# Second aggregation of a graph network kernel: edge tiles 1925 to 2050 counted on TensorE, 1075 tiles gathered in place of 1200

## What is computed

```
# L0: two SAGE convolutions with mean aggregation
deg_inv = 1 / max(deg, 1)                       # 0 where deg is 0
h = relu(x @ Ws1 + (segment_sum(x[src], dst) * deg_inv) @ Wn1 + b1)
h = h @ Ws2 + (segment_sum(h[src], dst) * deg_inv) @ Wn2 + b2
x = layernorm(x + h)
# L1: messages over the edges
ef  = (relu(edge_attr @ We1 + be1) @ We2 + be2) * sigmoid(edge_weight @ Wt + bt)
msg = relu(concat([x[src], ef]) @ Wm1 + bm1) @ Wm2 + bm2
out = layernorm(x + segment_sum(msg, dst) + x)
```

## Time and profile before

| what | us |
|---|---|
| median of 3 runs | 8275.95 |
| lowest and highest | 8274.34 and 8285.98 |
| profiled execution, its own time | 8290.47 |
| its span in the trace | 8288.8 |
| second stage in it, first gather to last window sum | about 2497 to 4070 |

### The profile page before, as it was taken

The page is one execution under the profiler, slowest core; times in us unless marked ns, Lnnn a source line. Parts: engine busy times, 40 slices in busy tenths (PEclk is TensorE's granted clock), DMA queues, the critical chain, the costliest instruction groups (busy, mean ns, idle before and its releaser), DMA issues.

```text
span 8288.8 us, 106834 instructions
## 1 busy us (share of the span) xinstructions
PE 6509.1 (79%) x34084; PEld 4100.4 (49%) x34084; DVE 4750.7 (57%) x8573; ACT 2462.6 (30%) x2998; POOL 5925.0 (71%) x5857
## 2 busy tenths in 40 slices
PE   5778777777776788887678888878888888888887
PEld 4555555444444555555444444444444444444444
DVE  8988877676755555555354444444444444444454
ACT  2111111111111000000134444444444444444444
POOL 7777665555547777777577777777777777777776
PEclk8889888888888999898799999999999999999998
DMA  4466666676758889898644444444444444444443
GB/s 122 154 201 223 228 231 227 232 240 219 249 190 285 290 298 309 303 318 305 216 124 125 130 127 127 129 123 128 126 128 126 129 127 130 125 128 129 128 129 98
DMA packets 598838, 1523.91 MB, mean 184 GB/s; under 512 B 157137, under 2 KB 290917, under 8 KB 587014
## 3 DMA queue, kind: packets, MB, share of 16 engines
q1 hardware_dynamic: 411075, 1133.17, 40.2%
q0 software_dynamic: 187200, 383.76, 16.7%
HBM read 1374.92 MB, written 141.47 MB: 183 GB/s over the span
## 4 chain that ended last, share of the span: by engine, by line
POOL 37%; issue 11%; PE 1%; DMA 1%; DVE 0%; POOLq 0%; ACT 0%; SPq 0%; DVEq 0%; ACTq 0%
POOL messages_rows L1704 37%; DMA messages_rows<-y_d,src_idx 1%; PE messages_p_msg L1785 1%; PE messages_p_msg L1788 0%; POOLq L1701 0%; DMA messages_sums<-in_message_base 0%; PE messages_win L1743 0%; PE messages_win L1761 0%; PE messages_win L1544 0%; DVE messages_below L1905 0%; DVE messages_parts L1895 0%; PE messages_p_edge L1800 0%; DVE messages_piece_stats L1559 0%; ACT messages_product L1833 0%; ACT L1536 0%
## 5 line engine op out<-in xcount | busy, mean ns | idle before, releaser
L1704 POOL DMA_INDIRECT messages_rows<-y_d,src_idx x3125 | 3190.2, 1021 | 1001.1 <-issue 944.5
L1110 POOL DMA_INDIRECT sum_x_rows<-in_x,sum_x_edges x1525 | 1568.5, 1029 | 855.8 <-PE sum_x_win L1200 428.3
L1900 DVE SCALAR_TENSOR_TENSOR messages_gated<-messages_p_edge,be,messages_gate 128x1024 f32<-128x1024 f32 x391 | 502.0, 1284 | 2138.8 <-PE messages_p_edge L1800 1039.3
L1110 POOL DMA_INDIRECT sum_z_rows<-z_d,sum_z_edges x1200 | 1165.0, 971 | 473.5 <-issue 419.2
L1785 PE MATMUL messages_p_msg<-messages_rows,identity 128*128 128x512 f32 x1564 | 963.2, 702 | 630.1 <-DMA messages_rows<-y_d,src_idx 611.5
L1788 PEld LDWEIGHTS messages_p_msg<-Wm_e,messages_gated 128*128 128x128 f32 x6250 | 937.6, 215 | 454.5 <-issue 454.5
L1212 PE MATMUL sum_x_build<-sum_x_key_hot,sum_x_low_hot 128*128 128x490 bf16 (+2 forms) x2900 | 837.0, 375 | 228.6 <-DVE sum_x_counts L1408 223.9
L1788 PE MATMUL messages_p_msg<-Wm_e,messages_gated 128*128 128x128 f32 x6250 | 929.2, 298 | 0.0
L1232 PE MATMUL sum_z_p_loaded<-sum_z_split,sum_z_counts 128*128 128x384 bf16 x2744 | 790.9, 346 | 155.1 <-DMA sum_z_split<-z_parts_d 149.9
L1820 ACT ACTIVATE messages_parts<-messages_p_msg 128x1024 bf16<-128x1024 f32 x391 | 399.7, 1022 | 1572.1 <-PE messages_p_msg L1788 1572.1
L1408 DVE SCALAR_TENSOR_TENSOR sum_x_counts<-sum_x_counts,sum_x_build 128x980 f32 (+3 forms) x635 | 647.8, 1020 | 360.6 <-PE sum_x_build L1212 348.5
(11 more groups left out here) (274 smaller groups left out, 9360.5 us busy)
## 6 DMA issues: line engine op xcount, KB each, us to landing
sum_x_split<-x_parts_d SPq DMA_DIRECT2D x392, 675.5 KB
sum_z_split<-z_parts_d SPq DMA_DIRECT2D x392, 675.5 KB
messages_when<-in_edge_weight SPq DMA_DIRECT2D x391, 512.0 KB
messages_attr<-in_span_attr SPq DMA_DIRECT2D x391, 256.0 KB, 3.1
counts_d<-sum_x_counts SPq DMA_DIRECT2D x28, 3136.0 KB
sum_z_counts<-counts_d SPq DMA_DIRECT2D x56, 1568.0 KB, 7.7
messages_rows<-y_d,src_idx POOLq DMA_INDIRECT x3125
sum_x_rows<-in_x,sum_x_edges POOLq DMA_INDIRECT x1525
```

Source lines behind the costliest of these rows:

```text
L1110: nc.gpsimd.indirect_dma_start(out=rows[:, s % depth, j, :], out_offset=None, in_=table, in_offset=bass.IndirectOffsetOnAxis(ap=edges[:, b ...
L1704: nc.gpsimd.indirect_dma_start(out=rows[:, g % SPAN_DEPTH, j, :], out_offset=None, in_=d["y"], in_offset=bass.IndirectOffsetOnAxis(ap=src_ ...
L1900: nc.vector.scalar_tensor_tensor(gated[:, g % SPAN_GATEDS, :], p_edge[:], t.be2[:, 0:1], gate[:, g % SPAN_GATES], ALU.add, ALU.mult).then_ ...
```

## The change

Tiles 1925 to 2050 are taken from the gathered to the counted ones. Their keys cover ten nodes, so a key table has 980 columns for 784 and the two build matmuls have 490 for 392. `sum_z_` builds 19 blocks for 13 and gathers 215 groups for 240. The tiles are to be built within 188 slots for 212, and 22 pieces for 20 are in the flat part.

```diff
-RUNS = (..., (1600, 1, 6), (1925, 1, 8))
+RUNS = (..., (1600, 1, 6), (1925, 1, 8), (2050, 1, 10))
...
     first = make_plan(m, 0, 1600, 28, 14, 290, SPACING)
-    second = make_plan(m, 1600, 1925, 13, 20, 212, SPACING_SECOND, first)
+    second = make_plan(m, 1600, 2050, 19, 22, 188, SPACING_SECOND, first)
```

More of the change, by code:

```diff
@@ L29 @@
 BANK_NODES = 5
-RUNS = ((300, 5, 5), (600, 3, 6), (750, 3, 8), (1050, 3, 10), (1200, 2, 8), (1500, 2, 10), (1600, 1, 6), (1925, 1, 8))
+RUNS = ((300, 5, 5), (600, 3, 6), (750, 3, 8), (1050, 3, 10), (1200, 2, 8), (1500, 2, 10), (1600, 1, 6), (1925, 1, 8), (2050, 1, 10))
 LONGEST = max(run for _, run, _ in RUNS)
```

## The result

| | before | after |
|---|---|---|
| median us, lowest to highest, 4 runs each | 8279.48 (8274.34 to 8285.98) | 8490.48 (8481.37 to 8494.56) |
| profiled execution, its own time | 8290.47 | 8494.56 |

The ratio of the times is 1.0253 with a 95% interval of 1.0235 to 1.0271. The change costs 211 us: slower, as forecast, inside the range, but 84 us above the forecast of 8406. Between the two profiled executions the spans differ by 203.9 us (8492.7 for the earlier trace rows).

What follows compares the result with a forecast made beforehand. Second-stage slots were bound closely together by gathers (6.37 us), TensorE's program order (6.78) and the chunk stream; 27 + 753 + 805 + 118 = 1703 us for 1573, so 130 us more: 8406 us, 8 in 10 range 8265 to 8500.

Steps and rivals of the forecast that it cites:

- start: Second stage from the first gather to the first pass: 26 us as now plus 1 us for the larger tables.
- first 16 passes: Slots 4 to 82 of the second stage: nine one-block passes at 44 us and seven two-block at 51, 753 us.
- slots 82 to 189: Late second stage with more builds per slot: 50 slots of 7.2 us and 57 of 7.8, 805 us.
- end: After slot 189: POOL's last 90 gathers, 114 us, and 4 us for the last window, 118 us.
- the gap: Between two passes, from last to next first product matmul: 9.2 or 10.7 us, holding half the counts and the first chunk.
- The lengths: Early passes without their gaps: 33.8 us with one block, plus 1 for piece traffic in the distance; 40 us with two.
- The marks of the second count halves: Sign that the forecast is right: these marks stand 43 to 53 us apart for the first 16 passes.
- the 0.95 or more: Sign that the forecast is right: DMA engines busy at least 0.95 in the first 16 passes, at about 350 GB/s.
- ten-node slots: Last 57 slots of slots 82 to 189, 2.2 tiles each: 7.8 us a slot; above 9 would show the forecast wrong.
- Ten-node part as slow as the first stage: Rival: ten-node slots take 9.7 us as TensorE and VectorE wait in turn, 108 us more, 8514 us; chance 0.14.
- Added work fits idle time: Rival: passes at the transfers' 41 us, late slots at the gathers' 6.37, 90 us less, 8186 us; chance 0.17.
- The stream is faster when asked: Rival: chunks move at 407 GB/s, early passes take 35.7 us, 571 for all sixteen, 8224 us; chance 0.06.

Runs made afterwards that it cites:

- run 3: Changed kernel with second-stage chunk loads, after the first three, cut to one slice of seven: 8375.29 us, 115 less than the changed kernel.
- run 8: Kernel before the change with chunk loads after the first three cut to one slice of seven: 8263.66 us against 8290.96 beside it.
- run 4: Changed kernel with VectorE's second-stage addition of counts cut to 14 of 98 slices: 8376.92 us, 114 less than the changed kernel.
- run 6: Changed kernel with the products of its last six blocks cut from 98 matmuls to 2 each, builds and chunk loads kept: 8472.39 us, 18 less.

## Why the prediction was right and where it was off

**Direction and place.** Right. Moving 125 tiles takes away 25 slots and lengthens the others. The stage took 208 us more (1781 for 1573), all else 4 us less (203.9 - 208).

**The terms**, from the cuts in the windows above:

| term | forecast | measured |
|---|---|---|
| start | 27 | 44 |
| first 16 passes | 753 | 825 |
| slots 82 to 189 | 805 | 787 |
| end | 118 | 125 |
| sum | 1703 | 1781 |

By the starts of the 17th and the 28th pass, which is what the forecast's terms meant, the last three are 815, 792 and 130: the sixteen passes missed by 62, and 10 us of the 72 in the table come from where I cut.

**Start: missed by 17.** I took it as 26 us and 1 us for the larger tables. In slot 2 VectorE runs a chain of short instructions for the places of the blocks (L280 to L312), 10.5 us here (2528.16 to 2538.62) and 9.9 in the kernel before (2521.29 to 2531.20). Everything that TensorE needs of VectorE stands behind it. Before, five builds stood ahead of the first product matmul at 2522.85, and TensorE met the chain behind it, in the first pass; now eight do, and it meets the chain ahead of the pass. TensorE's two waits, before and after, and part of the chain after:

```profile
2532.76 0.66 PE L1196 MATMUL sum_z_win<-sum_z_hot,sum_z_rows 128*128 128x64 f32 x2 [8.42 <-DVE sum_z_hot L976]
...
2541.90 0.81 PE L1212 MATMUL sum_z_build<-sum_z_key_hot,sum_z_low_hot 128*128 128x392 bf16 x2 [11.99 <-DVE sum_z_counts L1408]
...
2528.80 2.67 DVE L286 MEMSET sum_z_counts<- 1x44 f32 x20
```

So 12 of the 17 us are a wait that the kernel before has too, in its first pass (44.0 us long, for 37.0 now). The forecast left it out: its start is that of before, and its passes are copies of later ones.

**First 16 passes: the step that failed is the gap.** The lengths hold: 35.3 us for a forecast of 33.8 + 1, and 39.3 for 40. The gap was taken as 9.2 and 10.7 us, read at two passes at the start of the stage, with the reason that "half of the counts and the first chunk have to land in it". It was 13.9 behind both kinds, so the gaps cost 9 x 4.7 + 7 x 3.2 = 65 us, and the lengths came 2 or 3 us under: together the 62. Two things were wrong with it. The two rows were not typical: they hold no step of a piece, and over its first 16 passes the kernel before had 11.6 and 11.8, which alone makes 9 x 2.4 + 7 x 1.1 = 29 us. And the reason was wrong, so I let it stay where it grows. With the chunks cut to a seventh the gap did not move, in the changed kernel (run 3) or in the one before (run 8); with short additions it fell by 2 us (run 4). The other 36 us, 2.2 in each gap, come with the slots' other work: a gap now holds five builds where it held three. By the table of gaps TensorE's idle time in them is the same 5.3 us, of which more now ends with an addition (4.6 for 2.2) and next to none with a chunk (0.04 for 1.7), and its busy time grew by 2.3 us. Part of that is the clock and not the work. At the higher level the busy times would be some 6.3 x 0.84 = 5.3 and 8.6 x 0.73 = 6.3 us, an estimate from the table's rows, so about 1 us more work and about 1.3 us at the lower clock. No run separates the two. Of the length of a pass with two blocks I had the number and not the reason either: I set it by the transfers, and it is TensorE's own work. The marks of the second count halves came 46 to 55 us apart, for 43 to 53. The DMA engines stood at 0.86 over the stretch, not at the 0.95 or more that I had named as the sign: by run 3 transfers set only the passes with one block, 9 x 35.3 = 318 of the 815 us.

**Slots 82 to 189: right in sum, in part by luck.** 787 us for 805, 7.3 us a slot; VectorE was busy 558.58 of 787 us, 71% (forecast 60 to 70). TensorE's waits moved from chunks to additions as said. But ten-node slots were not the longer ones: timed by window sums they took 7.2 us from slot 131 on, where I had 7.8, and the eight-node slots before them 7.6, where I had 7.2. The two errors have opposite signs, some 19 us too little and 32 too much. The run with eight-node keys does not settle why, since it also moved tiles.

**End: 125 for 118.** A small miss.

**The rivals.** *Ten-node part as slow as the first stage* (9.7 us a slot): its time, 8514, is nearer to the result than the forecast, but its mechanism is excluded, these slots took 7.3. *Added work fits idle time:* excluded, late slots are 7.3 and not 6.37; run 6 shows the little that is true of it, TensorE's own matmuls for the six blocks are worth 18 us because VectorE's turn comes out under them. *The stream is faster when asked:* passes stood 49.2 and 53.2 us apart, not 35.7, and with six sevenths of every chunk load left out (run 3) the kernel still takes 96 us more than before (8375.29 for 8279.48), so a faster stream of chunks could not have made the change a gain. The Trainium skill, DMA: Bandwidth & Descriptors, section Bandwidth, has 425 GB/s for 16 MB at once and 341 for 1 MB; the first 16 passes moved 294 GB/s and 395 in 6 us of a gap, so no run tests the higher figure over a pass.

**Where the 211 us come from.** Not from one thing. The parts that runs measured, each alone:

- Waits for chunks that gathers covered before: cutting chunks gives 27 us in the kernel before and 115 in the changed one, nearly all of it in the nine early passes with one block. The difference is 88 us. Run 8 shows why: before, waits for gathered rows took the place of the waits for chunks.
- The builds of the 125 new tiles (key table, build columns, addition): 68 us by the time, of which 16 lie in the first sixteen passes, where the edit changes nothing; some 50 us.
- The products of the six new blocks: 18 us.

These are some 156 us, of single runs, and need not add. Some 55 us stay open. Three candidates are argued only: the 325 old tiles are built in fewer slots, the granted clock in the first part is 0.87 for 0.90 and in the early gaps 0.73 for 0.84, and at the start the wait described above is 3.6 us longer (12.0 for 8.4).

Single runs can be compared more closely by the stage alone, from the first gather to the last window sum in each trace, 1780.6 us in the changed kernel and 1571.7 in the one before. By it the cuts in the changed kernel took 128 us (chunks), 112 (additions), 266 (both), 20 (products) and 66 (builds), and the cut of the chunks in the kernel before took 41; the two orders turned round cost 47 and 65 us, and the second of them 21 in the kernel before. The difference that rests on two runs, 128 for 41, is 87 us and so the same as above.

## What to carry to other kernels

When one engine's pace (here POOL's gathers) covers the waits of the others, taking work from that engine removes the cover too: price every wait it hid, not just the work added. The same cut of the transfers was worth 27 us with the cover and 115 without it, because under the cover 103 us of waits for gathered rows came up in place of 141 us of waits for chunks. A term used sixteen times should be read as a mean over the stage and not at its first two places, and it is explained only when one knows all the work that stands in it: a wait for a transfer ended my gap, but it hid under the other work as soon as that grew. Where two engines take turns on one buffer, taking work from one of them gives back only part of it: 53 us of TensorE's matmuls gave 20, and some 360 us of VectorE's additions (489 to 127) gave 114. A stall that both kernels have can move from one term of the sum to another, as the chain of short instructions did here.

## What the runs showed that was not expected

Turning two orders round that looked wrong in the trace made the kernel slower each time: additions before key tables, 49 us; chunk loads ahead, 69 us, and 26 us in the kernel before. The granted clock fell to its lower level inside the gap shown above. Before it fell TensorE had done window sums and builds with waits between them, busy 2.35 of 5 us; it then stood at 0.50 from 2630 to 2640 us, and was back at 0.99 after the first 4 us of the pass's product matmuls. Such gaps are common: the sixteen early ones have a mean of 0.73. VectorE's addition of 980 columns took 1213 ns and that of 784 took 1038, so a quarter more columns cost it 17% more.
